# Layer-0 rounds: both pending candidate products right after the first block product, and A1 in two halves around S3

## The reference, cut to what matters

```
h = relu(layernorm(x));  x = x + adj @ (h @ W0) + b0             # layer 0
h = relu(layernorm(x))                                          # layer 1
for five steps:
    m = adj @ h
    z = sigmoid(m @ Wz + h @ U3 + bz);  r = sigmoid(m @ Wr + h @ U3 + br)
    h = (1 - z) * h + z * tanh(m @ Wv + (r * h) @ U5 + bv)
x = x + h
```

## Time and profile before

| | |
|---|---|
| median of 3 runs | 1631.22 us (1630.46 to 1631.99) |
| profiled execution, its own time | 1629.81 us |
| its span, first to last instruction | 1628.0 us |
| TensorE matmul busy | 1480.0 us, 91% |
| VectorE / ScalarE / GpSimd busy | 78% / 58% / 11% |
| mean granted TensorE clock | 0.968 of full speed |
| shares of the chain that ended last | TensorE 61%, VectorE 19%, ScalarE 10%, issue 6%, GpSimd 3% |

### The profile page before, as it was taken

One profiled execution on the slowest core, in us unless ns is written; L12 is line 12 of the kernel. 1 busy time (PEld: TensorE's weight loads), 2 busy tenths in 40 slices (PEclk: granted clock), 3 DMA queues, 4 the chain that ended last, 5 costly groups with the idle time before them and its releaser, 6 DMA issues.

```text
span 1628.0 us, 19931 instructions
## 1 busy us (share of the span) xinstructions
PE 1480.0 (91%) x6951; PEld 675.2 (41%) x6951; DVE 1263.5 (78%) x1689; ACT 951.0 (58%) x1470; POOL 181.0 (11%) x396
## 2 busy tenths in 40 slices
PE   4688999999897799999898889999989879999997
PEld 3343344344343344444443334434444434444443
DVE  8865877797687778778778678878778868778777
ACT  5536566765663565756475455666557365665664
POOL 1511003100213001200201300310020310000000
PEclk9899999999999999999999999999999989999999
DMA  4011243223132243224213133332321313322332
GB/s 171 1 26 30 52 91 62 49 56 65 40 88 43 46 94 78 58 55 67 59 34 90 30 88 78 65 65 46 71 46 44 87 30 83 67 55 56 68 59 78
DMA packets 317442, 100.57 MB, mean 62 GB/s; under 512 B 310304, under 2 KB 311200, under 8 KB 317344
## 3 DMA queue, kind: packets, MB, share of 16 engines
q1 hardware_dynamic: 315616, 98.64, 28.3%
q10 hardware_dynamic: 1728, 0.66, 0.2%
HBM read 16.39 MB, written 8.39 MB: 15 GB/s over the span
## 4 chain that ended last, share of the span: by engine, by line
PE 61%; DVE 19%; ACT 10%; issue 6%; POOL 3%; DMA 0%; ACTq 0%; SPq 0%; DVEq 0%; POOLq 0%
PE ps_a L580 20%; PE ps_c L580 11%; PE ps_u L624 5%; PE ps_u L628 5%; PE ps_u L626 5%; ACT ysc L820 5%; PE ps_b L580 4%; PE ps_v L624 3%; PE ps_v L626 3%; PE ps_v L628 3%; DVE area L1215 2%; DVE area L1219 2%; DVE nx_lo L1175 2%; DVE rh L1204 1%; DVE area L1221 1%
## 5 line engine op out<-in xcount | busy, mean ns | idle before, releaser
L580 PE MATMUL ps_a<-t_hi,nx_hi 128*128 128x512 f16 x640 | 250.1, 391 | 54.1 <-ACT rh L862 31.5
L580 PE MATMUL ps_a<-t_lo,nx_hi 128*128 128x512 f16 x640 | 250.0, 391 | 0.0
L580 PE MATMUL ps_a<-t_hi,nx_lo 128*128 128x512 f16 x640 | 250.0, 391 | 0.0
L871 ACT ACTIVATE m_hi<-rh 128x512 f16<-128x512 f32 x144 | 90.2, 628 | 164.6 <-DVE rh L1204 164.6
L862 ACT ACTIVATE rh<-ps_a 128x512 f32<-128x512 f32 x144 | 85.0, 590 | 158.0 <-PE ps_a L580 158.0
L1254 DVE TENSOR_TENSOR rh<-rh,area 128x512 f32<-128x512 f32 x160 | 109.3, 692 | 77.0 <-ACT rh L880 73.2
L1209 DVE SCALAR_TENSOR_TENSOR m_lo<-rh,m_hi 128x512 f16<-128x512 f32 x144 | 111.6, 779 | 73.6 <-ACT m_hi L871 68.5
L1215 DVE SCALAR_TENSOR_TENSOR area<-area 128x1024 f32<-128x1024 f32 x80 | 110.8, 1385 | 62.2 <-ACT area L875 62.2
L840 ACT ACTIVATE h_hi<-area 128x1024 f16<-128x1024 f32 x78 | 82.1, 1052 | 121.9 <-DVE area L1221 121.9
L875 ACT ACTIVATE area<-ps_v,bias,w_inv 128x512 f32<-128x512 f32 x160 | 123.9, 775 | 47.4 <-PE ps_v L628 47.4
L1258 DVE TENSOR_TENSOR rh_lo<-rh,rh_hi 128x512 f16<-128x512 f32 x160 | 110.0, 688 | 39.8 <-ACT rh_hi L893 38.6
(11 more groups left out here) (173 smaller groups left out, 3047.3 us busy)
## 6 DMA issues: line engine op xcount, KB each, us to landing
xr<-in_x_dram SPq DMA_DIRECT2D x8, 1024.0 KB, 5.2
out_dram<-xr SPq DMA_DIRECT2D x7, 1024.0 KB, 4.0
area<-in_adj_dram SPq DMA_DIRECT2D x8, 512.0 KB, 8.4
ysc<-in_x_dram SPq DMA_DIRECT2D x3, 1024.0 KB, 5.2
nx_hi<-s SPq DMA_TRANSPOSE x128, 2.5
nx_lo<-s SPq DMA_TRANSPOSE x128, 2.5
nx_hi<-h_hi SPq DMA_TRANSPOSE x96, 2.4
nx_lo<-h_lo SPq DMA_TRANSPOSE x96, 2.5
```

Of the source, the lines that this page charges most:

```text
L580: last = nc.tensor.matmul(o[:, :], a[:, PLACE[k], j, :], b[:, k, j, :], start=(opens and j == 0 and n == 0), stop=(j == HB - 1 and n == 2) ...
```

## The change: what it does

It touches the layer-0 rounds alone. On TensorE, in the six later rounds, `v_product` of quarter 1 moves from between S2 and S3 to directly behind that of quarter 2. In these six and in (0,1), the order S3, A1 becomes A1 (j = 0, 1), S3, A1 (j = 2, 3). The count of A1 rises with its second half, so it stays the fifth product counted. On ScalarE, `candidate` of quarter 1 moves up to directly behind that of quarter 2, ahead of `round_n`, `round_h` and the second evacuation. VectorE, GpSimd and SyncE keep their order, and no instruction is added or taken away.

```diff
-            def block_product(k, a_hi, a_lo):
+            def block_product(k, a_hi, a_lo, js=range(HB)):
                 opens, o = k in OPENS, P_BANK[k]
-                for j in range(HB):
+                for j in js:
...
-                last.then_inc(prod_done, 1)
+                if js[-1] == HB - 1:
+                    last.then_inc(prod_done, 1)
...
-            def layer_product(p, slot, k):
+            def layer_product(p, slot, k, js=range(HB)):
                 n = n_layer(p, slot)
-                bank_free(g_layer(p, slot), k)
-                pe.wait_ge(n_hi_done[0], split_count(n, k))
-                pe.wait_ge(n_lo_done[0], split_count(n, k))
-                block_product(k, ny_hi, ny_lo)
+                if js[0] == 0:
+                    bank_free(g_layer(p, slot), k)
+                    pe.wait_ge(n_hi_done[0], split_count(n, k))
+                    pe.wait_ge(n_lo_done[0], split_count(n, k))
+                block_product(k, ny_hi, ny_lo, js)
+
+            def rest_of_layer(p, slot):
+
+                layer_product(p, slot, K_S1)
+                layer_product(p, slot, K_S2)
+                layer_product(p, slot, K_A1, range(HB // 2))
+                layer_product(p, slot, K_S3)
+                layer_product(p, slot, K_A1, range(HB // 2, HB))
+                layer_product(p, slot, K_B1)
+                layer_product(p, slot, K_S4)
...
-                    for k in LAYER_ORDER[1:]:
-                        layer_product(0, 1, k)
+                    rest_of_layer(0, 1)
...
                     layer_product(p, slot, K_A0)
                     v_product(s, 2)
-                    layer_product(p, slot, K_S1)
-                    layer_product(p, slot, K_S2)
                     v_product(s, 1)
-                    for k in LAYER_ORDER[3:]:
-                        layer_product(p, slot, k)
+                    rest_of_layer(p, slot)
...
                     candidate(s, 2)
+                    candidate(s, 1)
                     if slot == 1:
                         round_n(p, 1, 0, 0)
                         round_n(p, 1, 0, 1)
                     round_h(s, 1, 0)
                     evacuate(g, s + 1, 1, LAYER_ORDER)
-                    candidate(s, 1)
```

## The result

The changed kernel takes 1632.84 us, the median of 16 runs (1631.23 to 1634.57). The kernel before takes 1630.5 us, also over 16 runs (1627.57 to 1632.26). The ratio is 1.0016 with a 95% interval of 1.0008 to 1.0023: slower by about 2.3 to 2.6 us, clear of noise, and under the 0.2% that I called no change. The profiled execution has a span of 1630.5 us against 1628.0, with a mean granted clock of 0.964 against 0.968.

A forecast was written before the change was run, and what follows sets the result against it. TensorE's work was taken to bound most of the time, with waits for VectorE and ScalarE between. Terms -0.9 - 0.8 + 3.6 = +1.9 us on 1631.22 gave 1633.1 us, range 1629.8 to 1636.3.

The forecast's parts named there:

- TensorE's own order: Six later rounds: covers behind S2 and S3 still hold with 0.44 us to spare, so reordering costs nothing.
- Round (0,1), -0.9: Round (0,1): half of A1 fills the gap before S3, so sum_m through next A0 come earlier; -0.9 us.
- Slot 0, -0.27 a round: Three slot-0 rounds: round_h starts 0.27 us earlier, most of 2.2 us lost in ScalarE's queue; -0.8 us in all.
- Slot 1, +1.2 a round: Three slot-1 rounds: early candidate delays round_n, VectorE and S4 by 1.2 us; +3.6 us in all.
- The clock, which I added at nothing: S4 in slot 1: longer wait may cost clock; nothing added, though 5.09 us for S4 would make the sum +4.8.
- the slower rival: Slot 1: all three S4 run wholly at half clock, 2.9 us in all, giving 1636.0 us; chance 0.20.
- four order terms: TensorE's reordering at nothing, round (0,1) -0.9, slot 0 -0.8 and slot 1 +3.6 us, summing to +1.9.
- the one in which the half-clock stretch swallows part of the delay: Slot 1: S4 has fewer slow matmuls, gaining back 0.6 us per round; +0.1, 1631.3 us; chance 0.20.
- the faster one: Slot 0: the whole 2.2 us reaches the statistics, 6.6 us over three rounds; sum -3.9, 1627.3 us; chance 0.08.

The follow-up runs named there:

- e1_halves_only: Kernel before with A1 in halves around S3 in all seven layer-0 rounds, candidate and its product left in place; 1628.74 us against 1629.62.
- e4: e3 with, in slot 0, the second round_h ahead of the third evacuation on ScalarE; 1628.33 us against 1629.62 for the kernel before.
- e3: Changed kernel with the candidate of quarter 1 behind both round_n on ScalarE in slot 1; 1628.36 us against 1629.62 for the kernel before.
- e5: e4 with S4's sums and three low parts of m first on VectorE, second round_h later on ScalarE, in slot 1; 1621.36 us, kernel before 1630.19.
- e8: Changed kernel without GpSimd's b0 bias add for slot 1 of groups 1 to 3, so output incomplete; 1612.53 us against 1630.19 before, two runs.
- e2: Kernel before with only the candidate products and candidate of quarter 1 early, S3 and A1 whole in old order; 1632.86 us against 1629.62.

## Why the prediction was right

The forecast was 1633.1 us, +1.9, and "the same". Measured were 1632.84 us and +2.3 to 2.6. The time came nearer than the difference because the kernel before measured 0.7 us less over 16 runs than over the three that the forecast started from.

- **TensorE's own order costs nothing.** Right. No TensorE wait for an evacuation before S3 or B1 shows in a later round of the changed kernel.
- **Round (0,1), -0.9.** Right: -0.82 at `sum_m` and at the next A0. e1_halves_only shows it alone, -0.9 by medians, within its noise.
- **Slot 0, -0.27 a round.** Right in size (wait 0.50 to 0.21) and in reason: e4 takes the queue away and the wait before S4 is gone. What it frees is lost to the clock until the waits are filled.
- **Slot 1, +1.2 a round.** Right. VectorE waits 1.12 us and S4 1.19 to 1.24 us more. e3 undoes this one delay and the loss is gone.
- **The clock, which I added at nothing.** This term was mis-sized. S4 took 5.09, 5.09 and 5.06 us against 4.28, 4.15 and 4.13: +2.7 us, where I had put nothing and the slower rival, to which I had given 0.20, had put 2.9. So the rival was right about S4 and wrong about the total, which came out near mine because other stretches went the other way. A0 behind the 7.03 us wait after round (0,1) took 3.91 us (window below) instead of 5.09. And of the three stretches that lie in the middle of groups, in two the half clock was in the kernel before and in one in the changed kernel.

Window of that A0 in the changed kernel:

```profile
106.86:110.77 3.91, 3.91 (x12) 1.52 (x13) 3.18 (x6) 0.77 (x2) 0.00 (x0) 0.65 0.49 100
```

Windows around the three stretches, first of the kernel before and then of the changed kernel (the clock is the third number from the end):

```profile
299.00:310.00 11.00, 8.31 (x37) 3.50 (x38) 9.29 (x10) 4.74 (x9) 3.23 (x1) 1.00 0.50 91
690.00:702.00 12.00, 8.84 (x33) 3.37 (x34) 8.22 (x9) 4.71 (x9) 3.71 (x1) 0.86 0.49 98
1084.00:1095.00 11.00, 8.37 (x32) 3.15 (x30) 8.32 (x9) 3.71 (x6) 2.37 (x1) 0.84 0.47 95
```

```profile
299.00:310.00 11.00, 8.37 (x32) 3.10 (x30) 8.15 (x10) 4.26 (x8) 1.51 (x1) 0.84 0.53 88
690.00:702.00 12.00, 8.24 (x37) 3.30 (x36) 9.27 (x10) 6.96 (x13) 4.51 (x1) 1.00 0.45 86
1084.00:1095.00 11.00, 7.24 (x33) 2.82 (x32) 8.12 (x9) 5.83 (x10) 4.51 (x1) 1.00 0.46 94
```

Nothing of the change touches these stretches, and each is worth some 1.6 us. With the starts of the same products set side by side in the two profiles, the +2.5 us between them close: +1.9 for the order, +2.7 for S4's clock, -0.9 up to the next wait behind the 7.03 us one, -1.4 for the three stretches, and +0.2 for B1 behind the slot-0 rounds and the clock behind S4 together. So the forecast of the sum was right, its four order terms were right one by one, and its closeness beyond that is chance: a clock term of 2.7 us was met by others of -2.1 us that I had not seen either. One profile each cannot say what these are on average; the median granted clock is 0.964 over the changed kernel's 16 runs and 0.965 to 0.967 over the runs of the kernel before beside the experiments, which points to a small cost on balance. Of the rivals, the one in which the half-clock stretch swallows part of the delay is refuted, and so is the faster one, by the 3.05 us in which VectorE stands idle.

## What to carry to other kernels

An instruction that is moved forward on a queue delays what it passes, so ask who waits for those. Here a result that nobody needed yet was put ahead of one that VectorE wanted at once, and one line moved back was worth 4 us. And cost a wait of TensorE at its length plus the half clock behind it: here filling waits of 5 us with idle matmuls gave 11 us, and it showed that an order worth 5 to 6 us had looked worth 1. Where S4's wait was taken away by reordering (e5), the wait mostly moved on, and what stayed was about the clock.

## What the runs showed of the hardware that I had not expected

- A wait of TensorE can cost more than its length, because the product behind it comes at half clock. At full clock the 12 matmuls take 2.60 us. Behind waits of 2.32 us (e8) they took 2.60 us, behind 5.4 us 3.96 to 4.68, behind 6.6 us 5.06 to 5.09. But behind 5.8 us they took 3.95 us once and 5.09 twice (e2), behind 4.94 us 5.09 three times of three in e4 and from 4.29 to 5.09 in e2, and behind 5.71 us 4.41 to 4.70 in the kernel before. So a shorter wait can cost more clock than a longer one, and the same wait can cost 1.4 us or 2.5. Why, these runs don't settle; only that with TensorE kept busy up to the last 0.6 to 1.0 us of the wait the product came at full clock, in every such window. B1 in the first and the third such round of e2_candidate_only, behind waits of 4.94 and 4.95 us:

```profile
423.88:428.97 5.09, 5.08 (x12) 1.79 (x13) 1.98 (x3) 2.57 (x4) 0.19 (x1) 0.50 0.01 2
...
1210.52:1214.81 4.29, 4.29 (x12) 1.62 (x13) 1.98 (x3) 2.56 (x4) 0.39 (x2) 0.60 0.00 0
```

- GpSimd's bias add (4.5 to 5.0 us) and its after-effect on the clock cost the changed kernel some 20 us, an estimate from e8's two runs, although GpSimd is busy for only 11% of the span.
